# Selective-scan block beside a quantised feed-forward: decay blocks moved to SBUF, four PSUM banks for transposed states, W_out kept by halves

## The reference, cut to what matters

```python
xn = layernorm(x)                         # x: 8 x 1024 x 512, float32
out = x + mamba(xn) + fp4_ffn(xn)

# mamba, for each of the 1024 channels d and 16 states s
xz = xn @ W_in;  x_branch, z = split(xz)
xc = silu(causal_conv4(x_branch) + conv_b)
B, C, dt = split(xc @ W_x);  dt = softplus(dt + dt_bias)
h[t] = h[t-1] * exp(dt[t] * A[d, s]) + (dt[t] * xc[t]) * B[t, s]
y[t] = sum_s h[t] * C[t, s]
mamba = ((y + xc * D_param) * silu(z)) @ W_out
```

## Time and profile before

| | |
|---|---|
| median of 3 runs | 5827.97 us (5827.87 to 5835.2) |
| profiled execution, its own time | 5827.07 us |
| its span | 5824.2 us |
| PE / DVE / ACT / POOL busy | 85% / 86% / 48% / 62% |
| granted TensorE clock, mean | 0.964 |
| phases `phase_w` and `phase_a` end, about | 1820 us |
| first scan to the last add of `phase_b` | 1935.6 to 5803.5 us |

### The profile page before, as it was taken

One profiled execution on the slowest core, in us unless ns is written; L12 is line 12 of the kernel. 1 busy time (PEld: TensorE's weight loads), 2 busy tenths in 40 slices (PEclk: granted clock), 3 DMA queues, 4 the chain that ended last, 5 costly groups with the idle time before them and its releaser, 6 DMA issues.

```text
span 5824.2 us, 78018 instructions
## 1 busy us (share of the span) xinstructions
PE 4979.6 (85%) x21764; PEld 3145.6 (54%) x21764; DVE 5035.1 (86%) x6343; ACT 2768.5 (48%) x4579; POOL 3627.0 (62%) x2810
## 2 busy tenths in 40 slices
PE   1799999999998688888888888888888888888867
PEld 1688888888885344444444444444444444444444
DVE  7666766666662699999999999999999999999998
ACT  1111111111111665666666666666666665666653
POOL 4333333333331687878778788787877878878785
PEclk9999999999999899999999999999999999999968
DMA  2111111111112122222222222222122222222111
GB/s 74 33 42 41 43 40 43 41 41 43 40 42 80 63 77 71 73 73 67 74 71 76 71 65 79 68 76 72 66 74 71 75 71 66 75 71 75 61 56 49
DMA packets 211700, 362.55 MB, mean 62 GB/s; under 512 B 26208, under 2 KB 58976, under 8 KB 207216
## 3 DMA queue, kind: packets, MB, share of 16 engines
q1 hardware_dynamic: 211312, 358.17, 19.9%
HBM read 287.80 MB, written 70.29 MB: 61 GB/s over the span
## 4 chain that ended last, share of the span: by engine, by line
DVE 32%; issue 14%; PE 12%; ACT 5%; POOL 3%; DVEq 1%; DMA 0%; ACTq 0%; SPq 0%; POOLq 0%
DVE hs L1095 20%; DVE acc L1109 11%; PE ht L1212 4%; PE mm L1201 4%; POOL v L919 3%; ACT decay L1056 2%; PE mm L1161 1%; PE mm L1152 1%; DVEq L794 1%; DVE rtb L1081 1%; PE mm L1169 1%; POOL dt L932 1%; ACT xc L981 0%; ACT L1056 0%; ACT dt L1036 0%
## 5 line engine op out<-in xcount | busy, mean ns | idle before, releaser
L919 POOL TENSOR_TENSOR v<-u,b_rep 128x512 f32<-128x512 f32 x2048 | 2578.4, 1274 | 706.7 <-DVE hs L1095 704.7
L1212 PEld LDWEIGHTS ht<-ident,hs 128*128 128x128 f32 x8192 | 957.2, 146 | 1879.8 <-DVE acc L1109 911.4
L1212 PE MATMUL ht<-ident,hs 128*128 128x128 f32 x8192 | 1361.2, 291 | 628.2 <-DVE acc L1109 577.4
L1056 ACT ACTIVATE decay<-dt,a_neg 128x512 f32<-128x512 f32 x2048 | 1376.5, 685 | 607.8 <-DVE hs L1095 586.3
L1109 DVE SCALAR_TENSOR_TENSOR acc<-ht,c_now,acc 128x512 f32<-128x512 f32 x2048 | 1483.7, 725 | 22.9 <-PE ht L1212 22.7
L1095 DVE TENSOR_TENSOR_SCAN hs<-decay,v 128x512 f32<-128x512 f32 x1024 | 1240.4, 1211 | 136.6 <-POOL v L919 111.7
L1095 DVE TENSOR_TENSOR_SCAN hs<-decay,carry,v 128x512 f32<-128x512 f32 x1024 | 1303.2, 1273 | 11.8 <-ACT decay L1056 6.3
L489 ACT ACTIVATE sg<-gate 128x512 f32<-128x512 f32 (+1 forms) x192 | 108.0, 563 | 1331.7 <-PE up L535 1331.7
L1152 PE MATMUL mm<-x_in,w_in 128*128 128x512 f32 x1024 | 527.6, 622 | 20.9 <-DMA x_in<-xnt_d 18.7
L1201 PE MATMUL mm<-w_out,yt 128*128 128x512 f32 x1024 | 536.5, 624 | 7.7 <-ACT xb L966 7.4
L1169 PE MATMUL mm<-w_in,x_z 128*128 128x512 f32 x1024 | 519.1, 610 | 0.0
(11 more groups left out here) (124 smaller groups left out, 6927.3 us busy)
## 6 DMA issues: line engine op xcount, KB each, us to landing
b_rep<-ssm_d SPq DMA_DIRECT2D x512, 256.0 KB, 3.4
tap_diag<-tap_d SPq DMA_DIRECT2D x128, 256.0 KB, 2.9
rtb<-res_d SPq DMA_DIRECT2D x128, 256.0 KB, 4.2
xt<-in_L_attn_x SPq DMA_DIRECT2D x64, 256.0 KB, 2.8
xnt_d<-xntb SPq DMA_DIRECT2D x64, 256.0 KB, 2.7
rt<-in_L_attn_x SPq DMA_DIRECT2D x64, 256.0 KB, 2.7
res_d<-rt SPq DMA_DIRECT2D x64, 256.0 KB, 2.0
x_in<-xnt_d SPq DMA_DIRECT2D x16, 1024.0 KB, 4.8
```

Source lines behind the costliest of these rows:

```text
L919: nc.gpsimd.tensor_tensor(v[k % 2][:, j, :], u[g][:, j, :], b_rep[k % 4][:, :], ALU.mult).then_inc(v_ready, 1)
L1056: nc.scalar.activation(decay[n % 4][:, :], dt[g][:, j, :], ACT.Exp, scale=a_neg[:, GD * g + j, s:s + 1]).then_inc(decay_ready, 1)
L1212: last = nc.tensor.transpose(ht[n % 2][:, j, :], h[k % 2][:, j, t * P:(t + 1) * P], ident[:, :])
```

## The change

It does four things in `phase_b`.

1. The four `decay` blocks become SBUF tensors. ACT writes them and DVE reads them there.
2. The PSUM banks that this frees become two more `ht` banks (four in all) and two new banks `tt`. PE's transposes now wait for `summed` of step `n - 4`.
3. The tasks `xd` and `yt` (the short turns, 4 transposes each) use `tt[0]` and `tt[1]` in turn. All other products keep `mm[0]` and `mm[1]`, in turn among themselves.
4. `w_out` holds one channel group (4 x 128 rows) instead of both. The one load at the start (2 MB) goes, and two loads of 1 MB per chunk come, at slots 2 and 15 of SP's table, each after the products with the other half (`wo_done`).

```diff
-    w_in, w_out = sb("w_in", [P, KH, 2 * DI]), sb("w_out", [P, ND, D])
+    w_in, w_out = sb("w_in", [P, KH, 2 * DI]), sb("w_out", [P, GD, D])
...
-    decay = [psum(f"decay{p}", [P, CL]) for p in range(4)]
-    ht = [psum(f"ht{p}", [P, GD, P]) for p in range(2)]
+    decay = [sb(f"decay{p}", [P, CL]) for p in range(4)]
+    ht = [psum(f"ht{p}", [P, GD, P]) for p in range(4)]
     mm = [psum(f"mm{p}", [P, 512]) for p in range(2)]
+    tt = [psum(f"tt{p}", [P, 512]) for p in range(2)]
...
+    turns = [m[1] in ("xd", "yt") for m in MM]
+    place_of = {m[1:]: sum(turns[n] == turns[i] for i in range(n)) for n, m in enumerate(MM)}
...
-    SP_AT = {2: [("load", 1, 0), ("load", 1, 1)], 5: [("tap", 2)], 7: [("tap", 3)], 8: [("store", 1, 0)],
+    SP_AT = {2: [("w_out", 1), ("load", 1, 0), ("load", 1, 1)], 5: [("tap", 2)], 7: [("tap", 3)], 8: [("store", 1, 0)],
...
-             15: [("store", 1, 3)], 16: [("tap", 6)], 17: [("tap", 7), ("x_in",)], 19: [("tap", 0)],
+             15: [("store", 1, 3), ("w_out", 0)], 16: [("tap", 6)], 17: [("tap", 7), ("x_in",)], 19: [("tap", 0)],
...
     def bank_of(*task):
-        return next(n for n, m in enumerate(MM) if m[1:] == task) % 2
+        return (tt if task[0] in ("xd", "yt") else mm)[place_of[task] % 2]
...
+    def had_bank(c, n):
+
+        of_kind = [i for i in range(len(MM)) if turns[i] == turns[n]]
+        at = of_kind.index(n)
+        for back in range(at - 2, -len(of_kind) - 1, -2):
+            owner, sem_, value = copied_out(c if back >= 0 else c.plus(-1), MM[of_kind[back % len(of_kind)]])
+            if owner.exists(NC):
+                return owner, sem_, value
+        return None, None, None
...
-        sp.dma_start(w_out[:, :, :], W_out.rearrange("(k p) n -> p k n", p=P)).then_inc(w_out_loaded, 16)
+        w_out_rows = W_out.rearrange("(k p) n -> p k n", p=P)
...
+            elif what == "w_out":
+                g, = args
+                o = c.plus(-g)
+                if o.exists(NC):
+                    wait(sp, wo_done, o.at(8, 4 * g))
+                    sp.dma_start(w_out[:, :, :], w_out_rows[:, GD * g:GD * g + GD, :]).then_inc(w_out_loaded, 16)
...
-            nc.vector.scalar_tensor_tensor(out=acc[g][:, t, :], in0=ht[n % 2][:, :, :].rearrange("p j d -> p (j d)"),
+            nc.vector.scalar_tensor_tensor(out=acc[g][:, t, :], in0=ht[n % 4][:, :, :].rearrange("p j d -> p (j d)"),
...
-                    if isinstance(c.q, int) and c.c == 0 and (g, t) == (0, 0):
-                        pe.wait_ge(w_out_loaded, 16)
+                    wait(pe, w_out_loaded, o.at(32, 16 * g + 16))
...
-            wait(pe, summed, c.at(128, n - 1))
+            wait(pe, summed, c.at(128, n - 3))
             for j in range(GD):
-                last = nc.tensor.transpose(ht[n % 2][:, j, :], h[k % 2][:, j, t * P:(t + 1) * P], ident[:, :])
+                last = nc.tensor.transpose(ht[n % 4][:, j, :], h[k % 2][:, j, t * P:(t + 1) * P], ident[:, :])
```

More of the change, by code:

```diff
@@ L740, in phase_b @@
             room -= 1
-    assert len(MM) % 2 == 0 and room >= 0
+    turns = [m[1] in ("xd", "yt") for m in MM]
+    place_of = {m[1:]: sum(turns[n] == turns[i] for i in range(n)) for n, m in enumerate(MM)}
+    assert sum(turns) % 2 == 0 and len(MM) % 2 == 0 and room >= 0
     ACT_AT = {4: [("silu_z", 1, 0), ("silu_z", 1, 1)],
@@ L957, in extra @@
                 i = args[0]
-                x, made = xb[i % 2], mm[bank_of("ip", i)]
+                x, made = xb[i % 2], bank_of("ip", i)
                 wait(act, cv_done, o.at(ND, i - 1))
@@ L975, in extra @@
                 wait(act, cv_done, o.at(ND, i + 1))
-                nc.scalar.activation(xc[:, i, :], mm[bank_of("cv", i)][:, :], ACT.Copy).then_inc(cv_copied, 1)
+                nc.scalar.activation(xc[:, i, :], bank_of("cv", i)[:, :], ACT.Copy).then_inc(cv_copied, 1)
                 return
@@ L986, in extra @@
                     wait(act, ssm_done, o.at(1, 1))
-                    nc.scalar.activation(ssm_sb[:, :], mm[bank_of("ssm")][0:NR, :], ACT.Copy).then_inc(ssm_copied, 1)
+                    nc.scalar.activation(ssm_sb[:, :], bank_of("ssm")[0:NR, :], ACT.Copy).then_inc(ssm_copied, 1)
                 else:
@@ L990, in extra @@
                     wait(act, ct_done, o.at(1, 1))
-                    nc.scalar.activation(c_next[:, :, :], mm[bank_of("ct")][:, 0:NT * NS].rearrange("p (t s) -> p t s", t=NT),
+                    nc.scalar.activation(c_next[:, :, :], bank_of("ct")[:, 0:NT * NS].rearrange("p (t s) -> p t s", t=NT),
                                          ACT.Copy).then_inc(ct_copied, 1)
@@ L1003, in extra @@
                 wait(act, z_done, o.at(8, 4 * g + t + 1))
-                nc.scalar.activation(sz[:, t, :], mm[bank_of("z", g, t)][:, :], ACT.Copy).then_inc(z_copied, 1)
+                nc.scalar.activation(sz[:, t, :], bank_of("z", g, t)[:, :], ACT.Copy).then_inc(z_copied, 1)
             elif what == "xs":
@@ L1013, in extra @@
                 nc.scalar.activation(acc[g][:, :, t * P:(t + 1) * P],
-                                     mm[bank_of("xd", g, t)][:, :].rearrange("p (t d) -> p t d", t=NT),
+                                     bank_of("xd", g, t)[:, :].rearrange("p (t d) -> p t d", t=NT),
                                      ACT.Copy).then_inc(acc_set, 1)
@@ L1018, in extra @@
                 wait(act, yt_done, o.at(8, 4 * g + t + 1))
-                nc.scalar.activation(yt[t % 2][:, :, :], mm[bank_of("yt", g, t)][:, :].rearrange("p (j d) -> p j d", j=GD),
+                nc.scalar.activation(yt[t % 2][:, :, :], bank_of("yt", g, t)[:, :].rearrange("p (j d) -> p j d", j=GD),
                                      ACT.Copy).then_inc(yt_copied, 1)
@@ L1080, in extra @@
                 wait(dve, wo_done, o.at(8, 4 * g + t + 1))
-                nc.vector.tensor_tensor(rt[t % 2][:, :], mm[bank_of("wo", g, t)][:, :], rt[t % 2][:, :],
+                nc.vector.tensor_tensor(rt[t % 2][:, :], bank_of("wo", g, t)[:, :], rt[t % 2][:, :],
                                         ALU.add).then_inc(added, 1)
@@ L1140, in products @@
             if unit == 0:
[L1142 to L1147, removed]
+                owner, sem_, value = had_bank(c, n)
+                if owner is not None:
+                    wait(pe, sem_, value)
+            bank, first, last = bank_of(*task[1:]), unit == 0, unit == UNITS[what] - 1
             if what == "ip":
@@ L1197, in products @@
                 if first:
-                    if isinstance(c.q, int) and c.c == 0 and (g, t) == (0, 0):
-                        pe.wait_ge(w_out_loaded, 16)
+                    wait(pe, w_out_loaded, o.at(32, 16 * g + 16))
                     wait(pe, yt_copied, o.at(8, 4 * g + t + 1))
-                made, done = nc.tensor.matmul(bank[:, :], yt[t % 2][:, j, :], w_out[:, GD * g + j, :],
+                made, done = nc.tensor.matmul(bank[:, :], yt[t % 2][:, j, :], w_out[:, j, :],
                                               start=first, stop=last), wo_done
```

## The result

The changed kernel takes 6833.74 us (median of 4 runs), the kernel before on the same chip 5827.92: a ratio of 1.1729, 95% interval 1.1714 to 1.1744. The profiled execution has a span of 6830.5 us at a mean granted clock of 0.895. I had forecast 7050 us, 6880 to 7450: the direction and the mechanism hold, but the forecast was 216 us too high, and the measured time lies 46 us under the range.

The account below looks back on a forecast made before the run. DVE, 98% busy, bounds the kernel before. Taking turns, POOL's 170 and DVE's 140 us plus 8 make 318 per chunk against 241.4; over 16 chunks 1226 us on 5827.07 gives 7050 us, range 6880 to 7450.

Parts of the forecast that it names:

- Exclusion: In `phase_b`, scans with two SBUF inputs and POOL instructions reading SBUF exclude each other, but for 0.15 us per hand-over.
- The other parts: `ht` and `tt` banks, ACT writing SBUF, scan length, `W_out` by halves, start load and clock: each taken as 0.
- The lead is mostly gone: POOL's eight-step lead over DVE is used up by 24 further operations against about 9 regains per chunk.
- The hand-over, 0.15 us: Overlap at each turn between DVE and POOL, leaving 1.12 us per multiplication and 1.09 per scan.
- The allowance of 8 us for idle stretches: Per chunk, added to 310 us for POOL waiting for ACT or DVE in its further operations, and for starts.
- The 24 further operations: POOL's operations per chunk besides its 128 multiplications, taken at 1.27 - 0.15 = 1.12 us each.
- The range: 8 in 10: 6880 us (hand-overs better by 0.01 each) to 7450, a little over the 339 us per chunk case.
- The signs: Profile after: steps every 2.3 to 2.5 us, longer records, POOL near 100% busy, `c_now` copies held, clock under 0.9.
- partial sharing: Rival: scans and multiplications slow each other but run together; 30% stretch gives 6000 us, 4%; 20% about 5830, 2%.
- scans that run beside POOL's reads: Rival: no exclusion for scans and PE waits go; say 5780 us, about 5650 with shorter scans; 7%.
- the dear end: Rival: POOL mostly at full lead, 339 us per chunk, 7390 us, or no hand-over gain, 352 us, 7596; 20%.

Follow-up runs that it names:

- the fill and the one-column multiplication: Changed kernel, each step's POOL multiplication replaced by a one-column multiplication and a constant fill: 5908.34 us; same replacement in the kernel before: 5816.65 us.

## Why the prediction was right in kind and wrong in size

- *Exclusion.* Right, and now shown for scans by the fill and the one-column multiplication. The other parts were costed at 0: `W_out` is measured at 0, and so are the banks, within some 10 us of noise (+1006.2 us without them and +1005.8 with them, each against the kernel before on its own chip). Where POOL does not hold it, a scan keeps its length with its decay in SBUF (in the run with one decay in four the shortest scan is 1.204 us with it and 1.191 with a decay in PSUM), so the gain of 0.065 us per scan that the prediction worked out as an estimate is not seen.
- *The lead is mostly gone.* Right: POOL never idles, and DVE waits 291 us for multiplications.
- *The hand-over, 0.15 us: the step that failed.* I read it as 0.14 to 0.16 from a few records of other operations in `phase_w`, and so had 1.12 us for a multiplication and 1.09 for a scan, 2.21 a step. In the changed kernel the record of a scan ends 1.07 us after that of the multiplication before it, and the record of a multiplication 1.08 us after that of the scan before it (means of 1920 each, from the records between 1946.7 and 6518.4 us). A step is 2.15 us. Without `carry` the hand-over is (1.21 + 1.27 - 2.15) / 2 = 0.17. With `carry` scans start as closely, though they are 0.06 longer alone, which makes it 0.20:

```profile
3463.20 1.57 DVE L1115 TENSOR_TENSOR_SCAN hs<-decay,carry,v 128x512 f32<-128x512 f32 x1
...
3465.34 1.58 DVE L1115 TENSOR_TENSOR_SCAN hs<-decay,carry,v 128x512 f32<-128x512 f32 x1
```

  I take it that what a scan with `carry` does at its start passes while it is held; no run tests this. 128 steps: -7.6 us per chunk.
- *The allowance of 8 us for idle stretches.* Wrong too: POOL is idle for 12.8 us in 15 chunks, under 1 us each. That is -8 us per chunk, as much as the hand-over. The lower end of the range was worked out without it, so it does not explain why the time fell below that.
- *The 24 further operations.* I had 1.12 each, as if a scan stood between any two POOL operations. Where the lead is gone, DVE waits through two or more of them that follow each other, with no hand-over between them. A POOL record that follows another one directly ends 1.24 us after it (mean of 356 in the 15 chunks, 24 a chunk). That is +2.9 us per chunk.
- *Sum.* From the records, 128 x 2.15 + 24 x 1.24 = 305; measured 304.8. Against the forecast, 318 - 7.6 - 8 + 2.9 = 305.3, and the rest is rounding.
- *The range.* Its lower end let the hand-over be 0.16 at most: 310 less 0.01 for each of 280, 307.2 us per chunk, or 6880 us. It was a floor only for a hand-over read from another pair of operations. Bounds of that one term from 0.13 to 0.20 would have given 14 us per chunk more room, 224 us in all.
- *The signs.* POOL's busy share, the clock under 0.9, DVE's missing waits for PE and the least distance of 1.05 us between ends came as said (the shortest is 1.06). Two did not. The steps are 2.15 us and not 2.3 to 2.5. And the copies of the C columns are hardly held any more, 0.36 us in the median where they took 1.10:

```profile
L1143 DVE COPY c_now<-c_next x16: 347/359/1195, 1946.7 to 6518.4; 128x64 f32<-128x64 f32 x16
```

- *A reading that does not hold in general.* From one copy in the kernel before I concluded that POOL does not lock a waiting DVE instruction out for more than one operation. For the scans this came out; for copies the run with eight more multiplications shows seven operations.
- *The rivals.* No partial sharing of the place was seen, nor scans that run beside POOL's reads, and the dear end did not come: it needed POOL at its full lead.

## What to carry to other kernels

Before a DVE operand moves from PSUM to SBUF, count the SBUF tensor inputs of the instruction: with the second one it takes turns with every POOL instruction that reads SBUF, and the time becomes the sum of both engines' work in place of the larger. A PSUM bank as one input is what lets DVE and POOL run side by side, and is worth more here than a spare bank for an engine that is early anyway. The count of inputs is not the whole rule: two operations with a single SBUF source and an SBUF result were held by POOL as well, the copy of 64 columns and L115 of `phase_w`. Look for short DVE copies with records far above their minimum: they tell that the two engines collide, before any change.

## What the runs showed that I had not expected

A two-input scan was let in after each single POOL operation, whereas the SBUF-to-SBUF copy of 64 columns could be held through seven in a row (8.67 us). In the kernel before, none of the 16 copies took more than 1.34 us, about one operation; what decides between the two was not tried. A held scan with `carry` takes no longer than one without. A fill of 128x512 on POOL takes 0.52 us and runs beside a scan from SBUF at full length.
